# Cross-attention and routed FFN on one Trainium2 core: Q, K and V as seven of eight block products (Strassen, one level), in two phases with K and V kept in DRAM

## Chip, cores and metric

The kernel runs on one core of a Trainium2 chip. Times are device microseconds (us) of that core; three timed runs of the kernel before are given. It is written by hand: each engine has its own instruction stream, and semaphores are the only order between them. The names used below are those of the profile: PE is TensorE's matmul, PEld its weight load, DVE is VectorE, ACT is ScalarE, POOL is GpSimd, SP is SyncE, which issues every DMA here.

## What is computed

The reference, cut to what matters (B = 8 batches of 128 tokens, D = 512, 32 heads of 128):

```python
h = rmsnorm(layernorm(x)) * ln_weight          # 1024 x 512
q = h @ w_q.T;  k = ctx @ w_k.T;  v = ctx @ w_v.T      # each 1024 x 4096, 32 heads of 128
score = q k^T + position_bias[head]            # per batch and head, 128 x 128
score = where(mask, score, -inf); p = where(mask, softmax(score), 0)
x1 = x + layernorm(x) + (p v) @ w_out.T
y = layernorm(x1)
r = softmax(y @ gate_w.T)                      # 8 experts
out = x1 + ((y * (r @ in_scale)) @ sign(weight).T) * (r @ out_scale) + bias
```

## The kernel before, in words

Everything is f32. A projection is made of three fp32r matmuls per 128 rows of the inner dimension: each operand is split into a high part (an fp32r copy, by ACT) and a low part (operand minus high part, by DVE or POOL), and `three` (L740) issues high x high, low x high, high x low into one PSUM bank. The inner dimension is 512, so one bank of 128x512 results takes 4 x 3 = 12 matmuls of 128x512.

`schedule()` (L44) writes out one list of steps by hand; every engine walks this list (`walk`, L248) and issues what it has in each step, in that order. A step waits only through semaphores, but an engine that waits in one step holds back all its later steps. The steps that matter here:

- ("Q", h, half), ("K", h, half): `project` (L773), 12 matmuls for one head and four batches, into `proj_bank`; ACT copies the bank out (`evacuate`, L407). ("V", group, tile): the same for four heads and one batch.
- ("WQ", h), ("WK", h), ("WV", g): SP loads raw weights, ACT makes the high part (L404), POOL the low part (L343), except for the first ones, whose low part DVE makes (L524, L530).
- ("S", h, half): four f32 score matmuls of 128x128, each shown as two (L821). DVE adds bias and mask (L591) and takes the row maxima (L594), POOL having summed bias and mask before (L354). ("EXP"): four exponentials on ACT (L428). ("N"): DVE divides by the row sums (L600 to L603). ("T"): four transposes on PE (L830), copied by ACT (L437). ("PV"): probabilities times values (L841); ACT takes the high part (L443), DVE the low part (L609). One such run from S to PV is called a unit: 64 units, four per pair of heads.
- ("OUT", pair, b): 6 matmuls of the output projection for a pair of heads and one batch, into `out_bank` (two banks in turn), which DVE adds to the accumulator `acc` (L619).
- ("LN"), ("RMS"), ("H"), ("X"): the norms of x, eight transposes on PE and their splits, all within the first 60 us. ("SIGN"), and everything after ("ST", 0): the FFN.

Q, K and V of head h+1 stand between the units of head h, so that the products cover the latencies of the softmax. A steady slot holds, in PE's order, Q, S, Q, S, K, two OUTs, K, T, V, PV, T, V, PV. The weights of each head and the values of four heads are double buffered in SBUF; nothing intermediate goes to DRAM.

```python
for n, ((left_hi, left_lo), (right_hi, right_lo)) in enumerate(pairs):
    pe.matmul(bank_tensor[:], left_hi, right_hi, start=n == 0, stop=False)
    pe.matmul(bank_tensor[:], left_lo, right_hi, start=False, stop=False)
    last = pe.matmul(bank_tensor[:], left_hi, right_lo, start=False, stop=n == len(pairs) - 1)
```

## Time and profile before

| what | value |
|---|---|
| median of 3 runs | 937.71 us (935.98 to 940.04) |
| profiled execution, first to last instruction | 936.0 us (its own time outside the span is not listed) |
| PE busy | 902.8 us, 96% of the span |
| DVE, ACT, POOL busy | 386.1, 382.1, 266.5 us |
| mean granted TensorE clock | 0.993 |
| chain that ended last: PE | 85% of the span, of which the three projection lines 54% |
| HBM read, written | 42.25 MB, 2.10 MB |

The profile is of one execution. Busy times of PE overlap: a 128x512 matmul is shown with some 0.39 us, while the next one starts 0.23 us after it. Work on PE is therefore counted below by the distance of starts, not by busy time.

### The profile page before, as it was taken

The numbers are of one execution on the slowest core, as the hardware profiler recorded it, in microseconds if no ns is written. First come the engines' busy times: TensorE is split into PE (matmuls) and PEld (weight loads), VectorE is DVE, ScalarE is ACT, GpSimd is POOL, SyncE is SP. The second block draws the span as 40 slices with busy tenths as digits, with TensorE's granted clock in tenths as the row PEclk, the third lists the DMA queues.
The fourth block names the chain that finished last, engine by engine and source line by source line (L and its number), as shares of the span: only waits on it lengthen the run. The fifth ranks groups of instructions, "written<-read, shape, count | busy, mean of one in ns | idle before, by whom it ended". The sixth has DMA issues, their size and how long they took to land.

```text
span 936.0 us, 12277 instructions
## 1 busy us (share of the span) xinstructions
PE 902.8 (96%) x4590; PEld 754.5 (81%) x4590; DVE 386.1 (41%) x666; ACT 382.1 (41%) x998; POOL 266.5 (28%) x183
## 2 busy tenths in 40 slices
PE   8789999999999999999999999999999999999898
PEld 7668888787888878787887878788787878888775
DVE  6943333334243233424233332423333242365784
ACT  6345334342433435252343435343353424354552
POOL 1452115131331314331151323313142311233152
PEclk9999999999999999999999999999999999999998
DMA  9120002010020101111020101201012100120002
GB/s 326 42 71 29 34 26 91 28 49 15 26 80 25 48 26 48 60 29 41 16 94 26 48 17 39 78 12 49 26 48 71 42 22 12 48 68 26 1 3 88
DMA packets 22330, 45.15 MB, mean 48 GB/s; under 512 B 2536, under 2 KB 6888, under 8 KB 21248
## 3 DMA queue, kind: packets, MB, share of 16 engines
q1 hardware_dynamic: 22272, 44.36, 14.6%
q8 instruction: 38, 0.62, 0.3%
q14 instruction: 20, 0.16, 0.1%
HBM read 42.25 MB, written 2.10 MB: 47 GB/s over the span
## 4 chain that ended last, share of the span: by engine, by line
PE 85%; DVE 8%; issue 3%; ACT 1%; DMA 1%; SPq 1%; DVEq 0%; ACTq 0%
PE proj L745 18%; PE proj L751 18%; PE proj L748 18%; PE o L841 6%; PE s L821 6%; PE out L745 5%; PE out L751 5%; PE out L748 5%; PE t L830 3%; DVE acc L619 2%; DVE probs_t L571 1%; DVE inv_sum L602 1%; DMA acc<-in_x 1%; PE proj L909 1%; PE proj L910 1%
## 5 line engine op out<-in xcount | busy, mean ns | idle before, releaser
L609 DVE TENSOR_TENSOR o_lo<-o,o_hi 128x512 fp32r<-128x512 f32 x64 | 44.2, 691 | 268.3 <-ACT o_hi L443 268.3
L354 POOL TENSOR_TENSOR bias_mask<-bias_raw,mask_neg 128x512 f32<-128x512 f32 x64 | 75.0, 1172 | 270.9 <-DVE probs L591 264.5
L428 ACT ACTIVATE probs<-probs,neg_max 128x128 f32<-128x128 f32 x256 | 99.7, 391 | 121.0 <-DVE neg_max L594 120.9
L619 DVE TENSOR_TENSOR acc<-out,acc 128x512 f32<-128x512 f32 x128 | 87.1, 688 | 83.9 <-PE out L751 82.7
L745 PE MATMUL out<-wo_hi,o_hi 128*128 128x512 f32 x256 | 104.3, 407 | 15.1 <-DVE acc L619 13.4
L745 PE MATMUL proj<-wv_hi,c_hi 128*128 128x512 f32 x256 | 106.5, 416 | 0.0
L745 PE MATMUL proj<-c_hi,wk_hi 128*128 128x512 f32 x256 | 103.7, 405 | 1.3 <-ACT c_hi L421 1.3
L745 PE MATMUL proj<-x_hi,wq_hi 128*128 128x512 f32 x256 | 103.9, 406 | 0.0
L343 POOL TENSOR_TENSOR wq_lo<-wq_raw,wq_hi 128x512 fp32r<-128x512 f32 x33 | 48.2, 1460 | 194.1 <-ACT wq_hi L404 194.1
L751 PE MATMUL proj<-wv_lo,c_hi 128*128 128x512 f32 x256 | 101.3, 396 | 0.0
L748 PE MATMUL out<-wo_hi,o_lo 128*128 128x512 f32 x256 | 101.0, 394 | 0.0
L751 PE MATMUL out<-wo_lo,o_hi 128*128 128x512 f32 x256 | 101.0, 394 | 0.0
L748 PE MATMUL proj<-c_hi,wk_lo 128*128 128x512 f32 x256 | 100.9, 394 | 0.0
L751 PE MATMUL proj<-c_lo,wk_hi 128*128 128x512 f32 x256 | 100.7, 393 | 0.0
L748 PE MATMUL proj<-wv_hi,c_lo 128*128 128x512 f32 x256 | 100.6, 393 | 0.0
L748 PE MATMUL proj<-x_hi,wq_lo 128*128 128x512 f32 x256 | 99.9, 390 | 0.0
L751 PE MATMUL proj<-x_lo,wq_hi 128*128 128x512 f32 x256 | 99.8, 390 | 0.0
L415 ACT ACTIVATE q_sb<-proj 128x512 f32<-128x512 f32 x64 | 37.5, 586 | 134.8 <-PE proj L751 134.8
L415 ACT ACTIVATE v_sb<-proj 128x512 f32<-128x512 f32 x64 | 38.2, 597 | 113.0 <-PE proj L751 113.0
L415 ACT ACTIVATE k_sb<-proj 128x512 f32<-128x512 f32 x64 | 37.4, 585 | 111.4 <-PE proj L751 111.4
L591 DVE TENSOR_TENSOR probs<-s,bias_mask 128x512 f32<-128x512 f32 x64 | 44.0, 688 | 82.8 <-PE s L821 82.8
L745 PEld LDWEIGHTS out<-wo_hi,o_hi 128*128 128x128 f32 x256 | 48.3, 189 | 30.1 <-issue 20.5
(111 smaller groups left out, 1570.4 us busy)
## 6 DMA issues: line engine op xcount, KB each, us to landing
wk_raw<-in_wk SPq DMA_DIRECT2D x33, 256.0 KB, 2.9
wq_raw<-in_wq SPq DMA_DIRECT2D x33, 256.0 KB, 2.6
wo_raw<-in_wo SPq DMA_DIRECT2D x16, 512.0 KB, 3.3
wv_raw<-in_wv SPq DMA_DIRECT2D x7, 1024.0 KB, 4.7
bias_raw<-in_pos_bias SPq DMA_DIRECT2D x33, 64.0 KB, 2.1
v_sb<-in_ctx_t SPq DMA_DIRECT2D x8, 256.0 KB, 6.1
acc<-in_x SPq DMA_DIRECT2D x2, 1024.0 KB, 9.4
out<-acc SPq DMA_DIRECT2D x8, 256.0 KB, 2.0
```

Of the source, the lines that this page charges most:

```text
L343: pool.tensor_tensor(lo[:], raw[:], hi[:].bitcast(F32), ALU.subtract).then_inc(done, 1)
L354: pool.tensor_tensor(bias_mask[:, n % 2], bias_raw[:, None, :].to_broadcast([P, HALF, P]), mask_neg[:, halves[half], :], ALU.add).then_inc ...
L415: act.activation(to, proj_bank[order % 2][:], ACT.Copy).then_inc(a_proj, 1)
L428: last = act.activation(probs[:, n % 2, b, :], probs[:, n % 2, b, :], ACT.Exp, bias=neg_max[:, col:col + 1], accum_out=row_sum[:, col:col ...
L591: dve.tensor_tensor(probs[:, n % 2], s_bank[n % 2][:].rearrange("p (b k) -> p b k", b=HALF), bias_mask[:, n % 2], ALU.add).then_inc(v_scor ...
L609: dve.tensor_tensor(o_lo[:, h % 2, part], o_bank[:], o_hi[:, h % 2, part].bitcast(F32), ALU.subtract).then_inc(v_olo, 1)
L619: dve.tensor_tensor(acc[:, b, :], out_bank[n % 2][:], acc[:, b, :], ALU.add).then_inc(v_acc, 1)
L745: pe.matmul(bank_tensor[:], left_hi, right_hi, start=n == 0, stop=False)
L748: pe.matmul(bank_tensor[:], left_lo, right_hi, start=False, stop=False)
L751: last = pe.matmul(bank_tensor[:], left_hi, right_lo, start=False, stop=n == len(pairs) - 1)
L821: last = pe.matmul(to[:, b * P:(b + 1) * P], q_sb[:, h % 2, toks], k_sb[:, h % 2, toks], start=True, stop=True)
L841: last = pe.matmul(to[:, b * P:(b + 1) * P], v_sb[:, group % 2, half * HALF + b, j * P:(j + 1) * P], probs_t[:, n % 2, b * P:(b + 1) * P], ...
```

## The change

Q, K and V are each computed by one level of Strassen's scheme in Winograd's form: the 512 inner rows and the outputs are cut in two halves, and of the eight block products seven remain, on sums of blocks of the activations and of the weights. One **group** is 4 blocks of 128x512 results (a pair of heads for Q and K, both halves of the tokens; or four times 128 tokens by 512 columns for V), made of 7 products of 6 matmuls each: 42 instead of 48. There are 16 groups each of K, V and Q, 48 in all.

The seven products of a group go into two PSUM banks, which accumulate over products: bank 0 takes products 1, 2, 7, 4, bank 1 takes 6, 5, 3; only 1, 7 and 6 start afresh. After each product one engine reads the bank: ACT after 1 and 2 (steps E1, C11), DVE after 6, 5, 7, 3, 4 (E6, E65, C22, C12, C21), adding to a tile of `ring`. The sums of weights are made by POOL on the raw weights (`pair_sums`, `value_sums`), the splits of the sums by ACT (high) and, for K and V, DVE (low); for Q POOL makes the low part. The sums of the context and of x are made once by DVE and POOL.

The kernel now has two phases. **Phase 1**: the 32 groups of K and V of all heads; a cycle is one group, with seven places for products (slots 0 to 6), in which products of group k (1 in slot 0, 6 in 2, 2 in 4, 5 in 6) alternate with the late ones of group k-1 (7 in slot 1, 3 in 3, 4 in 5). Even groups use `proj_bank`, odd ones `out_bank`. Each of the four result tiles is stored to DRAM (`save`); x is loaded, normed, transposed and split only in the last nine cycles, four tiles at a time, and its residual passes through DRAM (`x_load`). **Phase 2**: per pair of heads, K and V are loaded back (`keys_and_values`, 1 MB each, two tiles of each), and the 7 products of Q (for the pair after the next), 4 units and 8 OUTs are interleaved in 4 slots, one per unit.

The diff, cut to its core (the rest renames tiles and semaphores and gives the loads their new shapes):

```diff
-                    three(to, pairs, pe_proj, before)
+READ = {1: "E1", 2: "C11", 7: "C22", 4: "C21", 6: "E6", 5: "E65", 3: "C12"}
+FIRST_BANK = (1, 2, 7, 4)
+STARTS = (1, 7, 6)
...
+        new = {0: 1, 2: 6, 4: 2, 6: 5}
+        old = {1: 7, 3: 3, 5: 4}
...
+        put(k, 3, ("WL", m + 1))
+        put(k, 5, ("WS", m + 1))
+        put(k, 6, ("WX", m + 1, 0))
+        put(k + 1, 0, ("WX", m + 1, 1))
+        put(k + 1, 2, ("WX", m + 1, 2), ("WX", m + 1, 3))
...
+        put(k + 1, 0, ("VX", g, 5), ("VS4", g))
+        put(k + 1, 2, ("VX", g, 7))
+        put(k + 1, 4, ("VX", g, 3))
+        put(k + 1, 6, ("VX", g, 4))
...
+    put(k - 3, 3, ("LN", 0))
...
+    put(k + 1, 3, ("X", 3), *[("XL", i) for i in range(HALF, B)])
+    put(k + 2, 1, ("LN", 1))
...
+        return [*nxt, *early, *bias, *load, ("T", j), *middle, *norm, *extra, ("PV", j), *late]
...
+        elif p < LAST:
+            o = p - 1
+            steps += slot(j, outs(o, 3, 4), prod[1], outs(o, 5), [*split(1)])
+            steps += slot(j + 1, outs(o, 6) + prod[6], outs(o, 7), prod[2], [*split(2, 3)])
+        if p < LAST:
...
+            steps += slot(j + 2, prod[5] + prod[7], prod[3], [], [("WO", p), ("WOL", p + 1), *load])
+            steps += slot(j + 3, outs(p, 0) + prod[4], outs(p, 1), outs(p, 2), [("KV", p + 2), *sums])
+        else:
+            o = p - 1
+            steps += [("SIGN", c) for c in range(2)]
+            steps += slot(j, outs(o, 3, 4), outs(o, 5), [], [("SIGN", 2)])
+            steps += slot(j + 1, outs(o, 6), outs(o, 7), [], [("SIGN", 3), ("WO", p), ("SCALES",)])
+            steps += slot(j + 2, outs(p, 0), outs(p, 1), [])
...
+            def save(n, name):
...
+                sp.wait_ge(*read_done(name, n))
...
+                    sp.dma_start(k_spill[index[0]][:, i, j * HT:(j + 1) * HT], tile).then_inc(d_save[n % 3], 16)
...
+            def x_load(i):
+                if i >= HALF:
+                    sp.wait_ge(g_r, i - HALF + 1)
+                    sp.dma_start(r_spill[i - HALF], x_tiles[:, i - HALF]).then_inc(d_r[i % HALF], 16)
+                    sp.wait_ge(d_r[i % HALF], 16)
+                sp.dma_start(x_tiles[:, i % HALF], x[i]).then_inc(d_x[i % HALF], 16)
...
+            def pair_sums(m):
...
+                pool.tensor_tensor(w_stage[:, 4], w_stage[:, 0], w_stage[:, 5], ALU.subtract).then_inc(g_wsum, 1)
...
+                pool.tensor_tensor(w_stage[:, 1], w_stage[:, 6], w_stage[:, 4], ALU.subtract).then_inc(g_wsum, 1)
...
+            def c21(n):
+                dve.wait_ge(pe_prod, nth_product[n, 4])
+                dve.wait_ge(*read_done("E6", n))
+                dve.tensor_tensor(ring[:, n % 3, 2], banks_of(n)[0][:], ring[:, n % 3, 2], ALU.add).then_inc(v_read, 1)
...
+            def product(n, i):
...
+                to = take(banks_of(n)[0 if i in FIRST_BANK else 1])
...
+                three(to, pairs, pe_prod, i in STARTS)
+                read_by(to, *read_done(READ[i], n))
```

Three places of the order are needed later. On **PE**, in the steady part, from a transpose of probabilities to the product with the values; before, twelve matmuls of a V step stand between them (the three rows shown come four times):

```order
L830 MATMUL t<-ident,probs 128x128 x3
L745 MATMUL proj<-wv_hi,c_hi 128x512 [waits g_wv_lo,a_proj]
L748 MATMUL proj<-wv_hi,c_lo 128x512
L751 MATMUL proj<-wv_lo,c_hi 128x512
...
L841 MATMUL o<-probs_t,v_sb 128x128 [waits v_olo,a_proj,a_pt]
L841 MATMUL o<-probs_t,v_sb 128x128 x3
```

and in the changed kernel, third slot of the first pair of phase 2, with what follows:

```order
L1110 MATMUL t<-ident,probs 128x128 x3
L1049 MATMUL proj<-x_hi,w_hi 128x512 [waits g_wlo,v_read]
L1050 MATMUL proj<-x_hi,w_lo 128x512
L1051 MATMUL proj<-x_lo,w_hi 128x512
...
L1121 MATMUL o<-probs_t,v_first 128x128 [waits v_olo,d_v0,a_pt]
L1121 MATMUL o<-probs_t,v_first 128x128 x3
L1102 MATMUL s<-k_second,ring 128x128 [waits v_score,d_k1,a_read]
L1102 MATMUL s<-k_second,ring 128x128 x3
L1049 MATMUL out<-wo_hi,o_hi 128x512 [waits v_read,v_olo,g_wo_lo]
```

Six matmuls now stand between transpose and PV, and in this slot only the next unit's scores between PV and the first OUT that needs the low part of its result (v_olo).

On **DVE**, before, one head of the steady part:

```order
L594 TENSOR_REDUCE neg_max<-probs 128x4 [waits v_score]
L619 TENSOR_TENSOR acc<-out,acc 128x512 [waits v_acc,pe_out]
L600 RECIPROCAL inv_sum<-row_sum 128x4 [waits a_exp]
L602 TENSOR_TENSOR inv_sum<-inv_sum,row_valid 128x4 [waits v_chain]
L603 TENSOR_TENSOR probs<-probs,inv_sum 128x512 [waits v_chain]
L619 TENSOR_TENSOR acc<-out,acc 128x512 [waits v_acc,pe_out] x3
L609 TENSOR_TENSOR o_lo<-o,o_hi 128x512 [waits a_ohi] x2
```

and now, a cycle of phase 1 in which values are split (v_lo, L829) between the reads of the banks:

```order
L800 TENSOR_TENSOR ring<-proj,ring 128x512 [waits a_read,pe_prod]
L829 TENSOR_TENSOR v_lo<-big_stage,v_hi 128x1024 [waits a_vhi]
L813 TENSOR_TENSOR ring<-out,ring 128x512 [waits pe_prod]
L829 TENSOR_TENSOR v_lo<-big_stage,v_hi 128x1024 [waits a_vhi]
L818 TENSOR_TENSOR ring<-out,ring 128x512 [waits v_read,pe_prod]
L804 TENSOR_TENSOR ring<-proj,ring 128x512 [waits pe_prod]
L825 TENSOR_TENSOR w_lo<-w_stage,w_hi 128x256 [waits a_whi]
```

Reads of products (L800 to L818) are new on this engine, and the splits of K and V stand in the same queue; L818 is C21, the last read of a group's bank 0, behind a split of 1024 elements.

On **SP**, the changed kernel where the second half of x is loaded:

```order
L452 DMA v_spill<-ring 128x2x256 x2
L468 DMA r_spill<-early 128x512
L470 DMA early<-in_x 128x512
...
L452 DMA v_spill<-ring 128x2x256 x4
L427 DMA w_stage<-in_wk 128x2x256
```

The pair r_spill, in_x comes four times; each in_x waits until its r_spill has landed. Before, x came in two loads at the start.

## Rows read from the trace of the kernel before

**Rows 1.** Page, part 1: busy time, share of the span, instructions.
```profile
PE 902.8 (96%) x4590; PEld 754.5 (81%) x4590; DVE 386.1 (41%) x666; ACT 382.1 (41%) x998; POOL 266.5 (28%) x183
```

**Rows 2.** Stages: length, busy by engine (instructions), PE clock, DMA share, GB/s.
```profile
10.00:20.00 10.00, 10.00 (x43) 8.22 (x42) 8.33 (x19) 7.29 (x13) 0.00 (x0) 1.00 1.05 403
...
30.00:40.00 10.00, 7.54 (x37) 5.72 (x36) 8.96 (x16) 3.59 (x8) 5.52 (x4) 1.00 0.05 15
40.00:60.00 20.00, 15.64 (x80) 12.66 (x79) 13.01 (x16) 6.89 (x12) 7.88 (x7) 1.00 0.07 22
60.00:80.00 20.00, 17.91 (x89) 14.92 (x88) 7.62 (x11) 10.65 (x27) 8.93 (x5) 0.91 0.26 85
...
200.00:300.00 100.00, 97.94 (x503) 82.35 (x502) 34.29 (x56) 36.43 (x95) 26.80 (x18) 1.00 0.15 45
```

**Rows 3.** Waits: engine, line, releaser: us in total, times, longest.
```profile
PE out L745 <- DVE acc L619: 13.4, 13, 1.0
```

**Rows 4.** PE's timeline, steady part: start, duration, line, op, tiles.
```profile
337.85 0.39 PE L745 MATMUL proj<-c_hi,wk_hi 128*128 128x512 f32 x1
...
340.57 0.60 PE L830 MATMUL t<-ident,probs 128*128 128x128 f32 x4
340.92 0.48 PE L745 MATMUL proj<-wv_hi,c_hi 128*128 128x512 f32 x1
```

**Rows 5.** Timeline of the start.
```profile
5.30 1.28 ACT L421 ACTIVATE c_hi<-v_sb 128x512 fp32r<-128x512 f32 x2 [0.98 <-DMA v_sb<-in_ctx_t]
...
6.07 0.77 PE L745 MATMUL proj<-c_hi,wk_hi 128*128 128x512 f32 x1 [1.30 <-ACT c_hi L421]
...
10.47 0.63 PE L748 MATMUL proj<-c_hi,wk_lo 128*128 128x512 f32 x1
```

**Rows 6.** Groups by form: busy us, mean ns | idle before them.
```profile
L619 DVE TENSOR_TENSOR acc<-out,acc 128x512 f32<-128x512 f32 x128 | 87.1, 688 | 83.9 <-PE out L751 82.7
L343 POOL TENSOR_TENSOR wo_lo<-wo_raw,wo_hi 128x1024 fp32r<-128x1024 f32 x16 | 38.1, 2379 | 7.9 <-ACT wo_hi L404 7.9
L404 ACT ACTIVATE wk_hi<-wk_raw 128x512 fp32r<-128x512 f32 x33 | 20.6, 623 | 1.7 <-DMA wk_raw<-in_wk 1.7
L518 DVE TENSOR_TENSOR c_lo<-v_sb,c_hi 128x512 fp32r<-128x512 f32 x8 | 5.4, 692 | 2.2 <-ACT c_hi L421 2.2
L543 DVE BATCH_NORM_STATS2 stats<-acc 128x6 f32<-128x512 f32 x8 | 4.9, 677 | 1.0 <-DMA acc<-in_x 1.0
```

**Rows 7.** Page, part 6: DMA issues, KB each, median us to landing.
```profile
wk_raw<-in_wk SPq DMA_DIRECT2D x33, 256.0 KB, 2.9
...
out<-acc SPq DMA_DIRECT2D x8, 256.0 KB, 2.0
```

**Rows 8.** Line 603 (two SBUF inputs): duration ns min/median/max.
```profile
L603 DVE TENSOR_TENSOR probs<-probs,inv_sum x64: 691/693/1619, 65.9 to 879.8; 128x512 f32<-128x512 f32 x64
```

**Rows 9.** Timeline near the end: scores to exponentials, transpose to low part.
```profile
859.32 1.05 PE L821 MATMUL s<-k_sb,q_sb 128*128 128x128 f32 x8
...
860.41 0.69 DVE L591 TENSOR_TENSOR probs<-s,bias_mask 128x512 f32<-128x512 f32 x1 [2.92 <-PE s L821]
...
861.86 0.40 ACT L428 ACTIVATE probs<-probs,neg_max 128x128 f32<-128x128 f32 x1 [1.23 <-DVE neg_max L594]
...
865.71 0.60 PE L830 MATMUL t<-ident,probs 128*128 128x128 f32 x4
...
866.35 0.60 ACT L437 ACTIVATE probs_t<-t 128x512 f32<-128x512 f32 x1 [1.23 <-PE t L830]
...
868.63 0.60 ACT L443 ACTIVATE o_hi<-o 128x512 fp32r<-128x512 f32 x1 [1.68 <-PE o L841]
...
869.26 0.69 DVE L609 TENSOR_TENSOR o_lo<-o,o_hi 128x512 fp32r<-128x512 f32 x1 [0.83 <-ACT o_hi L443]
```

**Rows 10.** PE's timeline after an idle gap of the start.
```profile
67.60 0.66 PE L830 MATMUL t<-ident,probs 128*128 128x128 f32 x4 [2.09 <-DVE probs L603]
...
69.02 0.63 PE L748 MATMUL proj<-wv_hi,c_lo 128*128 128x512 f32 x1
```

1010 lines of the change are left out of this document (618 added, 392 removed), and 4 rows, old and new, of the table steps.

## The prediction

> **What bounds the kernel now.** I read the page's busy times first: PE is busy for 902.8 of 936.0 us, no other engine for more than 41% [rows 1]. The stages say the same in time: a stretch of 100 us in the middle has 97.9 us of PE and about a third each of DVE, ACT and POOL, and DMA at 45 GB/s, while an early stretch shows that 403 GB/s can be moved [rows 2]. The list of waits then gives PE's only steady loss: 13 waits of about 1.0 us for DVE's addition to `acc` [rows 3], one per pair of heads. So time falls by what PE no longer has to issue, and rises by each wait put in its way. The reader should see in PE's timeline what one matmul is worth: twelve of a K step lie between 337.85 and 340.57, that is 0.227 us each (2.72 / 12), not the 0.39 us of the duration [rows 4]. PE loses more than this only at the start. Its first matmul is at 6.07 us; the first twelve run at half clock (durations of 0.63 at 10.47) and cost 0.2 us more each [rows 5]; and from 30 to 80 us it idles 2.5, 4.4 and 2.1 us [rows 2], waiting for the norms of x. With about ten gaps whose edges hide 0.16 us each (0.39 - 0.23) and 1.8 us for the clock of 0.91 in 60 to 80, the start costs 6.1 + 2.4 + 8.9 + 1.6 + 1.8 = 20.8 us.
>
> **The change, part by part.**
>
> *Removed.* 48 groups of 6 matmuls less: 288 x 0.227 = **-65.4 us**. All were on PE's path. The distance should stay: operands are still 128x128 against 128x512, from the same kinds of tiles.
>
> *Reads of the banks.* 48 x 5 on DVE, at the 0.69 us of the nearest row, a PSUM bank added to an SBUF tile [rows 6]: 165 us of new DVE work. In phase 1 a cycle is 42 x 0.227 = 9.5 us of PE; DVE has 3.5 us of reads and, per K group, 2.4 us of low parts (0.35 + 3 x 0.69). It fits on average. What counts is who waits. Most banks have three slots (4.1 us) before PE wants them again. C21 has one: product 4 in slot 5, product 1 of the group after the next in slot 0, with only product 5 (1.36 us) between. After the last matmul DVE needs about 0.2 + 0.69 us, so the slack is 0.4 us. In the cycles where values are split, a low part of 1024 elements stands ahead of C21. I estimate it at 1.25 us, below two of the 512-element row [rows 6] (bounds 0.7 and 1.4), behind an ACT high part of 1.1 that waits for C11. DVE starts C21 some 1.6 us late: a stall of 1.1 us in three such cycles, 3.3 us. The same place is blocked once by the four statistics of x (2.7 us with what follows 3.0, [rows 6]): 1.8 us, once by a wait for a root, 0.3, and once by a split of x: 1.1. Sum **+6.5 us**.
>
> *The second half of x.* SP stores a residual tile, waits for it to land (2.0 us [rows 7]), then loads; four times that is about 9.4 us with the issues, and the last load lands 2.6 later. It starts in slot 3 of cycle 24; LN for it stands in slot 1 of cycle 25, where DVE then waits until about 8 us into the cycle. Behind it wait E6 and C12, and behind these PE's product 5. **+3.8 us**. SP's stores of results, queued behind, are late by one cycle at most, and the ring has three groups: nothing.
>
> *DRAM.* 33.5 MB more are written and as much read. Phase 1 moves about 175 GB/s (1 MB stored and 0.5 MB or more loaded per 9.5 us), phase 2 about 110, against 403 seen [rows 2]. The loads of K and V come one pair (some 30 us) ahead. Nothing, unless an issue on SP is held; the bounds are 0 and one 5 us wait at the turn of the phases.
>
> *Start.* The first product needs the first context block, 1.1 us of high part and 1.25 of low part: about 7.5 us. After that DVE must make 6 low parts and 2 sums of 1024 elements and 4 weight splits (12.4 us) before PE can finish group 0, and only then does SP load the weights of K pair 1, which need 2.9 us [rows 7] and their splits: 23.5 us. By 31.5 us I count 11 products done, 15.0 us of work: 16.5 lost. Now POOL: it has 6 operations of 1024 elements in this stretch, 2.4 us each [rows 6]. Line 603, whose inputs are both in SBUF, takes 0.69 us in the median but 1.62 at most [rows 8]; the addition from PSUM keeps 688 ns over 128 times [rows 6]. So a DVE operation with two SBUF inputs can be held by POOL, for what POOL has left. The bounds are nothing and all 14.4 us; I take 6.5, since half of the operations would meet each other. Start: 23 us against the 20.8 that it replaces, **+2.2 us**.
>
> The Trainium skill, "SBUF — State Buffer", section "Who interferes with whom", says that a VectorE instruction with two SBUF inputs and a GpSimd instruction that reads SBUF exclude each other for a whole instruction. That rule speaks against this change, which puts all low parts of K and V on DVE beside POOL's sums; the trace agrees as far as its 1.62 us go. Without it the sum would be 6.5 us lower.
>
> *Steady part of phase 2.* A pair is 42 x 0.227 + 48 x 0.231 + 4 x 2.2 (units) = 29.4 us of PE. I follow one slot. Scores start at 0; DVE adds the bias at 1.1, ACT begins the exponentials at 2.5 and ends at 4.1 [rows 9]. PE transposes the unit before at 3.6, ACT can copy at 4.2 (0.64 after [rows 9]), just after the exponentials; the copy ends at 4.9 and PV starts at 5.4, after six matmuls. The shorter cover holds with half a microsecond. The third slot does not: its last step is PV, then only the next scores (0.8 us) and then OUT, which needs ACT's high part (1.1 us after the start of PV, 0.6 long) and DVE's low part (0.69) [rows 9], behind a division that itself stands behind C12, or POOL's low part of the output weights (2.4 us [rows 6]). OUT starts about 1.4 us late, once per pair: 15 x 1.4 = 21, against 15 x 1.25 with its hidden edge now [rows 3]. **+2 us**. DVE's work per pair (22 us of 30) covers the rest.
>
> *Last pair.* It has no products of its own: 20.6 us of PE. Signs and scales (5 us of DVE) stand between its units, the copy of the second transpose waits for exponentials (3 us), the first OUT for the low part (3 to 4 us). Against about 1 us now: **+5 us**, bounds 2 and 9.
>
> Sum: 936.0 - 65.4 + 6.5 + 3.8 + 2.2 + 2 + 5 = 890.1 us of span. The median of the runs lies 1.7 us above the span of the profiled execution, so **892 us**.
>
> **The rivals.**
>
> *All cover holds* (the forecast's stalls are absorbed: DVE operations follow at 0.67 us, POOL is seldom in the way). For it: PE hardly ever waits now. Against: the slacks above are below a microsecond. Then only start and last pair remain: 936.0 - 65.4 + 2 + 1.7 = 874; 872 to 880.
>
> *The clock drops.* After an idle gap of 2.1 us the trace shows matmuls of 0.63 us from 69.02 on, eight in all, 1.6 us lost [rows 10]; the granted clock of that stage is 0.91 [rows 2]. If each pair's stall did this, and the start ran at half clock throughout (5 us), it would be 892 + 15 x 1.6 + 5 = 921. Against: the steady waits of 1.0 us now leave the clock at 1.00. The Trainium skill, "TensorE: Matmul & The Clock Gate", section "A second HAM failure mode: psum-queue depth-cycling", tells of a kernel whose short idles between PSUM groups made the clock swing; the stages from 200 to 300 us do not show it here.
>
> *Slower: every bank read late.* If DVE, with splits, reads and softmax in one queue, ran behind all the time, PE would wait at each of 64 units and 32 cycles, at the 1.0 us of the one such wait now known [rows 3]: 874 + 96 + 5 = 975 us. It is slower than before from 0.65 us per slot or cycle. Against: DVE's sums, 60% of a K or V cycle and 75% of a pair. For: C21's slack of 0.4 us is in every cycle.
>
> *The change does not do what it says*: not so; the order holds 2016 projection matmuls where 2304 were. What is left is one long wait that I have not seen, such as K and V arriving late for each pair; 2 us in each would give 922.
>
> **How the numbers follow.** Forecast 0.64 (880 to 905), all cover 0.13, clock or late loads 0.15 (905 to 930), slower 0.05, something between 0.03. About 0.5% is what a measurement can tell, 4.7 us. Leaving out under 2 in 10, the range runs from 874 to 915. Faster 0.93, same 0.02, slower 0.05.
>
> **What would show it.** Distances of 0.227 us between product matmuls; a pair of phase 2 about 31 us from S to S, and one wait of PE's OUT for DVE's o_lo or POOL's wo_lo of about 1.4 us in it; in phase 1 a wait of product 1 for DVE's L818 in the cycles with v_lo; LN's statistics waiting for in_x by about 5 us near 250 us; PE half idle until 30 us. Wrong would be a DVE busy above 90% of a phase, a granted clock under 0.95 beyond the start, or cycles of phase 1 longer than 10 us throughout.

## The result, and the profile after

The changed kernel takes **1065.95 us** (median of 4 runs, 1064.63 to 1066.31) against 938.12 us of the kernel before in the same set: a ratio of 1.137, with a 95% interval of 1.1345 to 1.1389. The forecast was 892 us, within 874 to 915. The sign was wrong, and the miss is 174 us.

The page of the changed kernel: busy times, tenths in 40 slices, and the chain that ended last.

```profile
span 1064.1 us, 12773 instructions
PE 901.9 (85%) x4302; PEld 737.5 (69%) x4302; DVE 673.7 (63%) x992; ACT 386.1 (36%) x987; POOL 377.2 (35%) x326
PE   2889789889797877678898889988998889888788
DVE  5846445546663755146676767676766776676786
PEclk7899989899898989689999899998999999999899
PE 51%; issue 16%; DVE 11%; POOL 10%; DMA 8%; ACT 3%; SPq 1%; ACTq 0%; POOLq 0%; DVEq 0%
```

PE's busy time is as long as before [rows 1], though 288 matmuls are gone: a matmul at half clock is shown with 0.63 us, not 0.39, and some 270 of them run so, against 36 before. With the 0.2 us that the prediction gives to each of these, the half clock is some 47 us of the 174 (an estimate, 234 x 0.2). The clock (PEclk) is below full nearly everywhere, and PE, 85% of the chain before, is 51% of it now. No other engine is full. So the time is in waits, and in the clock behind some of them. The list of waits names them (us in total, times, longest):

```profile
POOL w_stage L545 <- DMA w_stage<-in_wk: 166.0, 15, 30.5
ACT w_hi L672 <- DMA w_stage<-in_wk: 70.5, 15, 7.8
PE out L1049 <- issue: 50.5, 16, 4.4
PE proj L1049 <- DVE w_lo L825: 23.1, 6, 7.3
PE out L1049 <- DVE w_lo L825: 14.0, 4, 4.5
PE proj L1049 <- POOL w_lo L557: 13.1, 2, 6.9
DVE stats L855 <- DMA early<-in_x: 8.8, 3, 3.0
```

The 7.3 us in this list are before the very first product, at 12.1 us; the longest wait for a low part after the start is 6.9 us. "Issue" stands where the profile names no releaser.

I compare three times with the forecast: that of C21 (L818) of the first group, the distances of C21 through phase 1, and the length of a pair. The 36 us for the first are the nine products before it (12.3 us), the 23 us that the prediction gives to the start, and the read.

| stretch | forecast, us | measured, us | difference |
|---|---|---|---|
| start to C21 of group 0 | about 36 | 46.7 | +10.7 |
| 31 more cycles of K and V | 305.8 | 394.3 | +88.5 |
| Q0 and Q1 at the turn of the phases | 19.1 | 38.2 | +19.1 |
| 13 steady pairs | 13 x 30.8 | 13 x 35.0 | +54 |
| rest (turn to pair 1, last two pairs, FFN) | | | +2, a balance |
| sum | 890.1 | 1064.1 | +174 |

**Phase 1.** A cycle without a weight split at its edge takes 9.3 to 9.8 us, as forecast. The cycles in which two K groups stand back to back take 14 to 20 us. One of them in the timeline (start, duration, engine, line, in brackets the idle time before it and its releaser):

```profile
405.14 0.55 SPq L427 DMA_DIRECT2D w_stage<-in_wk  x1
405.73 0.59 SPq L428 DMA_DIRECT2D w_stage<-in_wk  x1
409.71 0.42 ACT L672 ACTIVATE w_hi<-w_stage 128x256 fp32r<-128x256 f32 x1 [4.69 <-DMA w_stage<-in_wk]
410.16 0.60 DVE L825 TENSOR_TENSOR w_lo<-w_stage,w_hi 128x256 fp32r<-128x256 f32 x1 [2.27 <-ACT w_hi L672]
410.91 0.47 PE L1049 MATMUL out<-c_hi,w_hi 128*128 128x512 f32 x1 [3.75 <-DVE w_lo L825]
```

There is one buffer `w_stage`. SP may issue the next load, in two halves, only when the last low part of the pair before is made; both halves have landed 4.6 us after the first issue, and then the high part, the low part and PE's product 1 follow one behind the other. PE waits 3.75 us here, up to 6.9 elsewhere.

Twice the landing itself is slow: the loads issued at 124.3 and 208.2 us take 6.9 to 7.6 us, behind 2 MB of V's weights that SP had issued 3 to 4 us before them. The cycles that follow take 16.7 and 16.0 us, and in them the late low parts of K also meet GpSimd's sums of V (start, duration; PE's wait in brackets):

```profile
138.39 2.69 POOL L563 TENSOR_TENSOR big_stage<-big_stage 128x1024 f32<-128x1024 f32 x1
138.78 2.85 DVE L825 TENSOR_TENSOR tail_lo<-w_stage,tail_hi 128x512 fp32r<-128x512 f32 x1
142.88 0.80 PE L1049 MATMUL proj<-v_hi,c_hi 128*128 128x512 f32 x1 [3.11 <-DVE ring L818]
```

**Phase 2.** The third slot of a pair:

```profile
627.46 1.06 PE L1121 MATMUL o<-probs_t,v_first 128*128 128x128 f32 x8
627.88 2.35 POOL L618 TENSOR_TENSOR wo_lo<-wo_raw,wo_hi 128x1024 fp32r<-128x1024 f32 x1 [4.13 <-ACT wo_hi L748]
628.47 1.78 DVE L913 TENSOR_TENSOR inv_sum<-inv_sum,row_valid 128x4 f32<-128x4 f32 x1
630.19 1.15 POOL L613 TENSOR_TENSOR bias_mask<-bias_raw,mask_neg 128x512 f32<-128x512 f32 x1
630.29 1.60 DVE L914 TENSOR_TENSOR probs<-probs,inv_sum 128x512 f32<-128x512 f32 x1
631.81 0.68 DVE L921 TENSOR_TENSOR o_lo<-o,o_hi 128x512 fp32r<-128x512 f32 x1
632.59 0.47 PE L1049 MATMUL out<-wo_hi,o_hi 128*128 128x512 f32 x1 [3.18 <-issue]
633.37 0.60 PE L1049 MATMUL out<-wo_hi,o_hi 128*128 128x512 f32 x1
633.76 0.63 PE L1050 MATMUL out<-wo_hi,o_lo 128*128 128x512 f32 x1
```

DVE's division (L913 on 4 elements, then L914) runs beside two operations of POOL: L913 ends when the first does, and L914 has most of its own 0.69 us still to do when the second has ended. The low part of the output (L921) stands behind it and ends at 632.49, and the first OUT of the pair, which needs it, starts at 632.59 after a wait of 3.18 us; POOL's wo_lo had been ready since 630.23. Eight matmuls at half clock follow, two of which are shown. The row before for L914's work is the 0.69 of [rows 8].

### The profile page after: what moved, and what is told of

It reads as the page before. It is cut to its first block, busy times and chain, and to the rows that moved or that the text cites. A ratio compares the mean times of both kernels' runs of the same rounds, so it can differ in the third digit from the quotient of the medians.

```text
span 1064.1 us, 12773 instructions
## 1 busy us (share of the span) xinstructions
PE 901.9 (85%) x4302; PEld 737.5 (69%) x4302; DVE 673.7 (63%) x992; ACT 386.1 (36%) x987; POOL 377.2 (35%) x326
## 4 chain that ended last, share of the span: by engine, by line
PE 51%; issue 16%; DVE 11%; POOL 10%; DMA 8%; ACT 3%; SPq 1%; ACTq 0%; POOLq 0%; DVEq 0%
PE out L1049 9%; PE out L1051 8%; PE out L1050 8%; PE proj L1049 5%; PE proj L1050 5%; PE proj L1051 5%; DMA w_stage<-in_wk 4%; POOL wo_lo L618 4%; POOL w_lo L557 3%; PE o L1121 3%; PE s L1102 3%; POOL bias_mask L613 2%; DVE w_lo L825 2%; PE t L1110 2%; ACT w_hi L672 2%
## 5 line engine op out<-in xcount | busy, mean ns | idle before, releaser
L557 POOL TENSOR_TENSOR w_lo<-w_stage,w_hi 128x256 fp32r<-128x256 f32 (+1 forms) x64 | 72.7, 1145 | 173.3 <-ACT w_hi L672 173.0
L1049 PE MATMUL proj<-x_hi,w_hi 128*128 128x512 f32 x210 | 94.2, 449 | 13.2 <-POOL w_lo L557 13.1
L672 ACT ACTIVATE w_hi<-w_stage 128x512 fp32r<-128x512 f32 (+1 forms) x120 | 66.4, 568 | 100.8 <-DMA w_stage<-in_wk 70.5
L825 DVE TENSOR_TENSOR w_lo<-w_stage,w_hi 128x512 fp32r<-128x512 f32 (+1 forms) x56 | 50.3, 908 | 61.6 <-ACT w_hi L672 61.6
L1050 PE MATMUL proj<-x_hi,w_lo 128*128 128x512 f32 x210 | 88.2, 420 | 0.0
L1051 PE MATMUL proj<-x_lo,w_hi 128*128 128x512 f32 x210 | 86.7, 413 | 0.0
L1049 PE MATMUL proj<-c_hi,w_hi 128*128 128x512 f32 x112 | 50.7, 453 | 36.8 <-DVE w_lo L825 23.1
L914 DVE TENSOR_TENSOR probs<-probs,inv_sum 128x512 f32<-128x512 f32 x64 | 71.6, 1118 | 2.2
L618 POOL TENSOR_TENSOR wo_lo<-wo_raw,wo_hi 128x1024 fp32r<-128x1024 f32 x16 | 38.2, 2385 | 75.8 <-ACT wo_hi L748 75.8
L921 DVE TENSOR_TENSOR o_lo<-o,o_hi 128x512 fp32r<-128x512 f32 x64 | 43.8, 684 | 28.2 <-ACT o_hi L742 28.2
L1051 PEld LDWEIGHTS out<-wo_lo,o_hi 128*128 128x128 f32 x256 | 52.2, 204 | 12.5
L1050 PEld LDWEIGHTS out<-wo_hi,o_lo 128*128 128x128 f32 x256 | 52.2, 204 | 6.8
```

Source lines behind the costliest of these rows:

```text
L557: pool.tensor_tensor(lo, w_stage[:, STAGED[part]], hi.bitcast(F32), ALU.subtract).then_inc(g_wlo, 1)
L618: pool.tensor_tensor(wo_lo[:], wo_raw[:], wo_hi[:].bitcast(F32), ALU.subtract).then_inc(g_wo_lo, 1)
L672: act.activation(hi, w_stage[:, STAGED[part]], ACT.Copy).then_inc(a_whi, 1)
L825: dve.tensor_tensor(lo, w_stage[:, STAGED[part]], hi.bitcast(F32), ALU.subtract).then_inc(v_wlo, 1)
L914: dve.tensor_tensor(probs[:, j % 2], probs[:, j % 2], inv_sum[:, cols, None].to_broadcast([P, HALF, P]), ALU.mult).then_inc(v_probs, 1)
L921: dve.tensor_tensor(o_lo[:, h % 2, part], o_bank[:], o_hi[:, h % 2, part].bitcast(F32), ALU.subtract).then_inc(v_olo, 1)
```

## The experiments

Theories: **A**, the reload of the single weight buffer is late; **B**, GpSimd's operations hold VectorE's; **C**, idle waits lower the clock and so cost twice; **D**, the first OUT of a pair has too little work over its latency. A result without a range is the time of one run, so differences of a few us between two such results are not told apart; the kernel before took 934 to 940 us beside all of them. Savings are against the 1066.0 us of the changed kernel unless another is named.

### One part taken away

```diff
             def pair_weights(m):
+                if m:
+                    return
...
-                    act.wait_ge(d_w, 32 * (m + 1))
+                    act.wait_ge(d_w, 32)
```

> Only the weights of the first pair of K heads are loaded for Q and K; all later pairs reuse them, so the weights (and the 16 MB of loads) of the 31 other pairs are left out, and POOL's sums wait for the low parts alone. Theory A (the single weight buffer: the load of the next pair is issued late, lands 4 to 8 us later, ACT and DVE wait for it in order and PE behind them): PE's waits for DVE's w_lo (some 37 us) and for POOL's w_lo (some 18 us) and the half-clock matmuls behind them go, 1066 becomes about 1000, and cycles of phase 1 where K groups stand back to back fall from 15 to 20 us to about 10 to 11. Rival B (VectorE is held by GpSimd's operations while both read SBUF): the low parts stay as slow as they are, only the DMA's share goes, 1045 or more.

**1012.8 us**, 53 less: between the two expectations, nearer to A's. C21 of the last K group comes at 396.8 in place of 441.0; PE's waits for low parts of weights fall from some 55 to some 29 us. The back-to-back cycles take 10 to 14 us, and those of Q1 and Q2 16 and 17. A is the largest single cause of phase 1; pairs stay at 35 us. The edit takes away the late issue and the slow landing together and does not tell them apart.

```diff
-                pool.tensor_tensor(w_stage[:, 4], w_stage[:, 0], w_stage[:, 5], ALU.subtract).then_inc(g_wsum, 1)
+                c = slice(0, 2 * P if not m else 8)
+                pool.tensor_tensor(w_stage[:, 4, c], w_stage[:, 0, c], w_stage[:, 5, c], ALU.subtract).then_inc(g_wsum, 1)
...
```

> GpSimd's sums of weights of K, V and Q are cut to 8 columns from the second pair and the second group of V on (the rest of those sums is left out); all semaphores stay. Theory B (VectorE's low parts of 0.7 to 1.25 us take 2.8 to 3.4 us beside GpSimd's sums): no low part over 1.5 us in phase 1 after 60 us, and 1066 becomes 1025 to 1040. Theory A (the loads are late): the waits for the low parts stay, since GpSimd's 4 sums (3 us) are only the tail of a wait of 5 to 8 us; 1050 to 1060. Phase 2 should change by less than 10 us by either.

**1046.6 us**, 19 less: between the two expectations, a little nearer to A's. The two cycles behind the load at 124.3 us fall from 16.7 and 12.0 to 11.1 and 9.2 us, and those with a late load and no sums of V beside it nearly stay (15.9 and 15.4 us become 15.0 and 15.6). The cycle of 16.7 us fell to 11.5 with one load as well: there the two causes are links of one chain.

```diff
...
-                pool.tensor_tensor(wo_lo[:], wo_raw[:], wo_hi[:].bitcast(F32), ALU.subtract).then_inc(g_wo_lo, 1)
+                c = slice(0, D if not p else 8)
+                pool.tensor_tensor(wo_lo[:, :, c], wo_raw[:, :, c], wo_hi[:, :, c].bitcast(F32), ALU.subtract).then_inc(g_wo_lo, 1)
```

> In phase 2 GpSimd's low parts of the Q weights and of the output weights and its sums of bias and mask are cut to 2 or 8 columns (the rest is left out), semaphores stay; phase 1 is as it was. Theory D1 (GpSimd's long operations hold VectorE and come late themselves: wo_lo, 2.4 us, stands in the third slot of each pair): the wait of the first OUT of a pair (3.2 us) and the half clock after it go, a pair falls from 35 to about 31 us, 1066 becomes about 1005. Rival D2 (the order: only one score stands between PV of the third unit and the first OUT, so that ScalarE's high and VectorE's low part of the output are late by themselves): the wait stays at 1.4 to 2 us, a pair is 33 to 34 us, 1035 to 1050.

**1004.6 us**, 61 less, as D1 said: a pair takes 30.6 us and the wait of the first OUT 0.65 us in the steady pairs, less than the 1.4 of the forecast. So GpSimd's operations beside it are what made the slot longer than forecast. Two successive C21 show the pair, and the stage from 600 to 700 us the clock (columns as in [rows 2]):

```profile
615.30 0.69 DVE L821 TENSOR_TENSOR ring<-proj,ring 128x512 f32<-128x512 f32 x1 [0.71 <-PE proj L1054]
646.00 0.69 DVE L821 TENSOR_TENSOR ring<-proj,ring 128x512 f32<-128x512 f32 x1 [0.71 <-PE proj L1054]
600.00:700.00 100.00, 98.05 (x557) 83.90 (x556) 68.33 (x121) 50.46 (x157) 15.62 (x42) 1.00 0.28 99
```

### The order mended in phase 2

```diff
-            steps += slot(j + 1, outs(o, 6) + prod[6], outs(o, 7), prod[2], [*split(2, 3)])
+            steps += slot(j + 1, outs(o, 6) + prod[6], outs(o, 7), prod[2], [*split(2, 3), ("WO", p), ("WOL", p + 1)])
...
-            steps += slot(j + 2, prod[5] + prod[7], prod[3], [], [("WO", p), ("WOL", p + 1), *load])
-            steps += slot(j + 3, outs(p, 0) + prod[4], outs(p, 1), outs(p, 2), [("KV", p + 2), *sums])
+            here = [("WO", p), ("WOL", p + 1)] if p == 0 else []
+            steps += slot(j + 2, prod[5] + prod[7], prod[3], [], [*here, *load])
+            steps += slot(j + 3, prod[4] + outs(p, 0), outs(p, 1), outs(p, 2), [("KV", p + 2), *sums])
```

> Full computation. Product 4 of Q stands before the first OUT of the pair instead of behind it, and the split of the output weights stands one slot earlier. If the cover of the first OUT is what is short (1.4 us more of PE work now lies over it, and wo_lo is out of the way), the wait of 3.2 us falls below 1 us and the matmuls behind it run at full clock: a pair of 31 to 32 us, about 1015. If VectorE is simply late as a whole (it is held by GpSimd in every slot), the wait moves to another place in the pair and the time stays above 1050.

**999.2 us**, 67 less, and more than expected. No wait is left in a steady pair, which takes 29.8 us: the 29.4 of PE's work in the forecast and 0.4. The same stage has PE busy throughout at full clock:

```profile
614.55 0.68 DVE L819 TENSOR_TENSOR ring<-proj,ring 128x512 f32<-128x512 f32 x1
644.30 0.68 DVE L819 TENSOR_TENSOR ring<-proj,ring 128x512 f32<-128x512 f32 x1
600.00:700.00 100.00, 100.00 (x570) 85.98 (x569) 73.28 (x123) 52.13 (x164) 51.69 (x44) 1.00 0.30 104
```

POOL is as busy here as it would be in any correct version, so it need not be taken away: the edit moves its 2.4 us to a place where nobody waits, and puts 1.4 us more of PE's work over the chain of the output. Which of the two steps gave how much was not separated.

### What a removed matmul is worth

```diff
+                    if order > 24 and order % 2:
+                        pairs = pairs[:3]
```

> The kernel before, with 9 instead of 12 matmuls in every second projection step from the 25th on, so one quarter of the inner dimension is left out there; nothing else changes. There are 192 projection steps, 84 of them are cut: 252 matmuls fewer. If removed matmuls are worth their distance, 0.227 us, the time falls by 57 us, to about 882. If the kernel before were bound by something that PE's busy time hides (the chain per head, or the reads of the banks), it falls by less than 40.

**892.8 us**, 47.1 less where 57 were expected. The group of OUT's first matmuls shows the rest (busy, mean ns, idle before it):

```profile
L745 PE MATMUL out<-wo_hi,o_hi 128*128 128x512 f32 x256 | 104.4, 408 | 24.2 <-DVE acc L619 22.4 <-issue 1.7
```

That wait was 13.4 us [rows 3] and is 22.4: with less work between the OUTs they wait longer. 47.1 + 9.0 = 56.1, that is 0.223 us for each of the 252; PE's other waits are as long as before to within 0.5 us. The first term of the forecast holds, and a part of it is lost where matmuls were cover.

### VectorE beside GpSimd, alone

```diff
+                    last = pool.tensor_tensor(pool_out[:, i], xt[:, 4:6], xt[:, 6:8], ALU.subtract)
...
+                    return dve.tensor_tensor(v_out[:, i], xt[:, 0:2], xt[:, 2:4], ALU.subtract)
```

> None of the computation is done: six copies each of five VectorE instructions alone, then beside six GpSimd additions of 1024 elements, both inputs of GpSimd in SBUF. Theory B (an instruction of VectorE with two SBUF inputs and one of GpSimd exclude each other): alone 1024 elements take about 1.2 us and 512 take 0.69; beside GpSimd (2.4 us each) they wait for it, 2 us or more on average, and the form from PSUM plus SBUF keeps 0.69, a form with one input keeps its time. Whether a 4-element instruction is held (1.6 us at times in phase 2) shows in the last group. Rival: they only share the bandwidth: every form, one input too, becomes some tens of per cent longer and none takes over 2 us.

Runs of one form each (start, time of all, count). L72 has two SBUF inputs of 1024 elements, L74 of 512, L76 a PSUM and an SBUF input, L78 one SBUF input of 512, L79 one of 4; the first row is VectorE alone, the others are beside GpSimd:

```profile
11.62 7.02 DVE L72 TENSOR_TENSOR v_out<-xt 128x1024 f32<-128x1024 f32 x6
21.84 9.91 DVE L72 TENSOR_TENSOR v_out<-xt 128x1024 f32<-128x1024 f32 x3
27.36 9.88 POOL L59 TENSOR_TENSOR pool_out<-xt 128x1024 f32<-128x1024 f32 x3
46.21 8.31 DVE L74 TENSOR_TENSOR v_out<-xt 128x512 f32<-128x512 f32 x3
65.64 6.79 DVE L76 TENSOR_TENSOR v_out<-ps,xt 128x512 f32<-128x512 f32 x11
70.50 9.25 POOL L59 TENSOR_TENSOR pool_out<-xt 128x1024 f32<-128x1024 f32 x4
88.36 10.00 DVE L78 TENSOR_SCALAR v_out<-xt 128x512 f32<-128x512 f32 x4
106.61 9.20 DVE L79 TENSOR_SCALAR v_out<-xt 128x4 f32<-128x4 f32 x7
```

With two SBUF inputs VectorE's instruction of 1024 elements takes 3.3 us beside GpSimd and 1.2 alone, and GpSimd's takes 3.3 as well, against 2.3 beside the form from PSUM: they take turns, and each is shown with the other's time. The form from PSUM keeps its 0.6 to 0.7 us (the first of the 11 in its row still run alone). Against my expectation the form with one SBUF input is held too (2.5 us against 0.4), and so is one of 4 elements: in turn one takes 2.3 us, about GpSimd's own, and the next 0.16, which is 1.3 on average. What is paid is the rest of GpSimd's instruction, not a share of one's own size. The Trainium skill, "SBUF — State Buffer", section "Who interferes with whom", has both cases, the second as a mode of `tensor_scalar` that uses two ports; the times agree with it, though the trace does not show the mode.

### The order mended in phase 1

```diff
+            order = order + v[0:1] + KEYS[k:k + 1] + v[1:2] + KEYS[k + 1:k + 2] + v[2:4] + KEYS[k + 2:k + 3]
...
-        put(k, 3, ("WL", m + 1))
+        e = k - 1 if 2 <= m < NPAIR and at[KEYS[m - 1]] < k - 1 else k
+        put(e, 3, ("WL", m + 1))
```

> Full computation. The order of the first 24 groups of phase 1 never has two K groups behind each other, and the load of a pair's weights is issued a cycle earlier where there is one to spare; the edit of phase 2 (product 4 before the first OUT, the split of the output weights a slot earlier) is kept, with which the time was 999.2. Theory A (the load of the single weight buffer is late where K groups stand back to back): the cycles of 15 to 17 us of the first 24 groups fall to 10 to 12, five of them, so 25 to 30 us less: about 972. Those from K12 to Q1 stay at 15 to 20. If the splits of V's weights, held by GpSimd's sums, make these cycles long (rival B), they stay above 13 us, and the time above 985.

**964.6 us**, 34.6 less than the 999.2 of the order mended in phase 2, which is kept here. From the second to the 24th group the cycles are 9.3 to 13.0 us long; those from K12 to Q1 keep their 12 to 21. A again.

The next kernel moved all of phase 1's sums and low parts to VectorE:

```diff
-                pool.tensor_tensor(w_stage[:, 4], w_stage[:, 0], w_stage[:, 5], ALU.subtract).then_inc(g_wsum, 1)
+                dve.tensor_tensor(w_stage[:, 4], w_stage[:, 0], w_stage[:, 5], ALU.subtract).then_inc(g_wsum, 1)
...
-                pool.tensor_tensor(big_stage[:, 4], big_stage[:, 2], big_stage[:, 3], ALU.add).then_inc(g_vsum, 1)
+                dve.tensor_tensor(big_stage[:, 4], big_stage[:, 2], big_stage[:, 3], ALU.add).then_inc(g_vsum, 1)
```

> Full computation. As the kernel with the new order of groups and the later OUT, and in phase 1 all sums and low parts of context, weights and x stand on VectorE, none on GpSimd: about 1.2 us instead of 2.4 to 3.3 for 1024 elements, and no collision. Theory B: VectorE does more and still ends earlier; the start is 5 to 8 us shorter, the cycles with splits lose 1 to 2 us each, about 950 to 960. Rival (VectorE's queue is what is full, not its port): the start becomes 5 us longer and the reads of the banks come late: 975 or more.

**965.2 us**: no difference, so neither expectation. The start is 0.6 us shorter and the first cycle 2.2, but those of K12 to K14 are 1.2 to 2.0 longer (16.95 in place of 15.0). I read this as the pair's sums now standing in VectorE's queue behind the wait for the load; that was not tested.

### The clock alone

```diff
+                if b == 0 and p < LAST:
+                    for _ in range(10):
+                        pe.matmul(take(out_bank[n % 2])[:], x_hi[:, 0, 0, 0:P], x_hi[:, 0, 0, :], start=True, stop=True, skip_group_check=True)
                 pe.wait_ge(g_wo_lo, p + 1)
```

> The changed kernel with ten matmuls more (128x512, into the bank that the first OUT of a pair takes and overwrites) before the waits of that OUT, in 15 pairs; all else as in the change. They fill 2.3 of the 3.2 us in which PE waits there. Theory C (it is the idle wait that lets the granted clock fall, and the half-speed matmuls behind it cost 2.4 us per pair on top of the wait): no matmul of 0.63 us behind the first OUT, a granted clock of 1.00 in the stages of phase 2, a pair of 32 to 33 us in place of 35, about 1030 in all. Rival: the clock falls for what PE did over the whole pair, or the 2.4 us are not additional (the products behind would wait anyway): 1060 or more.

**1047.7 us**: 18 less for 150 matmuls more, in the middle between the 1030 of C and the 1060 of its rival. A pair takes 33.2 us, 1.8 less, and the granted clock is 1.00 from 500 to 800 us; in the changed kernel it is 0.95 in the stage shown:

```profile
655.46 2.52 PE L1130 MATMUL out<-x_hi 128*128 128x512 f32 x10
658.92 0.47 PE L1049 MATMUL out<-wo_hi,o_hi 128*128 128x512 f32 x1 [0.94 <-issue]
600.00:700.00 100.00, 97.19 (x546) 82.62 (x545) 73.66 (x113) 45.62 (x141) 45.42 (x40) 1.00 0.28 99
```

C is shown for the pairs: nothing that the OUT waits for was changed, and only the clock behind it has. Of the 5.6 us that a pair had over its work, at least 1.8 are the clock and 3.2 the wait itself. The 13 steady pairs alone gain 23 us; from C21 of the last Q group to the end this run takes 5 us longer than the changed kernel, and why was not followed.

### Small edits towards a better version

Each of these is made to the kernel of 964.6 us or its successor. First, ScalarE's first bank read moved forward:

```diff
-    steps = [("WARM",), ("WS", 0), ("CX", 1), ("WX", 0, 0), ("CX", 2), ("WX", 0, 1), ("CT", "T3"), ("CT", "T1"), ("CX", 7),
+    steps = [("WARM",), ("WS", 0), ("CX", 1), ("WX", 0, 0), ("CX", 2), ("WX", 0, 1), *product(0, 1)[:2], ("CT", "T3"), ("CT", "T1"),
+             ("CX", 7), ("P", 0, 2), ("C11", 0), ("CT", "T2"), ("WX", 0, 2), ("CX", 6), ("CT", "T4"), ("CX", 5), ("WX", 0, 3),
```

> Full computation; to the kernel of 964.6 us (groups alternated, OUT later) one edit: ScalarE reads the bank after the first product of the first group as soon as its queue has the second split of the context, not behind all seven splits, and the second product follows. Theory: PE's wait of 10.5 us for that read (from some 13 to 22 us) is due to its place in ScalarE's queue; the second product comes some 8 us earlier, later products then wait for the splits, and the start is 3 to 8 us shorter: 957 to 962. Rival (VectorE's low parts set the start): under 2 us.

**967.5 us**: nothing gained. The 10.5 us wait went, and one of 7.8 us for DVE's L807 and others of 1.7 and 2.3 us for its low parts stand in its place. VectorE's low parts set the start, as the rival had it. Then the load in two halves:

```diff
+            def first_weights(m):
+                if m:
+                    for part in range(2):
+                        sp.wait_ge(*low_done(m - 1, part))
+                    sp.wait_ge(g_wsum, 4 * m)
+                sp.dma_start(w_stage[:, 0:3:2], w[2 * (m % NPAIR)].rearrange("p (b c) d -> p b (c d)", b=2)).then_inc(d_wa, 16)
```

> Full computation; to the kernel of 964.6 us one edit: the raw weights of the first head of a pair are loaded as soon as the first two splits of the pair before are done, by a DMA of their own, and only those of the second head after the last split. Theory A (late loads into the single buffer are what the cycles from K12 to Q1 of 12 to 20 us consist of): product 1 no longer waits for the load (5 us), the wait moves to product 6, which has 1.4 us more cover, and the six cycles lose 2 to 4 us each: 945 to 952. Rival (the chain of sums, high and low parts is as long by itself): under 5 us less, 960 or more.

**956.6 us**, 8 less than 964.6: just under the 960 of the rival, and short of theory A's 945 to 952. Two cycles fell from 16 and 15 to 12.5 us, the others changed by 1.4 at most. Both edits together:

> Full computation; groups alternated, OUT later, early read and split load together. If their gains add (7 and 16 us), about 942, within 1% of the kernel before (938 to 940); if the rivals hold for both, 960.

**957.8 us** (957.6 to 960.7), ratio to the kernel before 1.0224, interval 1.0203 to 1.0244: the early read adds nothing. It was left out of what follows.

With the three causes taken away at once (loads, sums, the order of phase 2; the same edits as above):

> The changed kernel with three edits together: weights of Q and K loaded once (those of the other pairs are left out), GpSimd's sums cut to 8 columns (the rest of the sums left out), and the order of phase 2 with the later OUT. If the loads, the sums on GpSimd and the cover of the first OUT are nearly all of what the forecast missed, their savings add or do better where one hid the other: 1066 - 67 - 53 - 19 = 927 or less, down to 905, with cycles of phase 1 of 9.5 to 11 us from 60 us on except the one in which VectorE waits for the second half of x. If a fourth cause of size is hidden behind them (the reads of the banks, DRAM traffic of the results), 940 or more.

**928.8 us**, 137 less: almost the sum of the single savings (139), just above what the three causes alone would give and well under the 940 of a fourth of their size. The 31 cycles take 342.1 us in place of 394.3, and Q0 and Q1 23.9 in place of 38.2. The cycle near 300 us keeps its 18.9, and nine late cycles take 11 to 14 us. That cycle is the second half of x; in the changed kernel:

```profile
317.53 1.65 SPq L468 DMA_DIRECT2D r_spill<-early  x1
320.98 0.35 SPq L470 DMA_DIRECT2D early<-in_x  x1
321.37 0.43 SPq L468 DMA_DIRECT2D r_spill<-early  x1
325.13 0.33 SPq L470 DMA_DIRECT2D early<-in_x  x1
328.05 0.69 DVE L855 BATCH_NORM_STATS2 stats<-early 128x6 f32<-128x512 f32 x1 [3.02 <-DMA early<-in_x]
328.71 0.33 SPq L470 DMA_DIRECT2D early<-in_x  x1
335.21 0.69 DVE L855 BATCH_NORM_STATS2 stats<-early 128x6 f32<-128x512 f32 x1 [2.92 <-DMA early<-in_x]
336.44 0.69 DVE L800 TENSOR_TENSOR ring<-out,ring 128x512 f32<-128x512 f32 x1
337.18 0.80 PE L1049 MATMUL out<-c_hi,w_hi 128*128 128x512 f32 x1 [7.89 <-DVE ring L800]
```

Store, wait, load takes 3.6 to 4.2 us a tile, and DVE follows tile by tile with a read of the bank (L800) behind it, for which PE waits 7.89 us. The next run mends it in the kernel of 956.6 us:

```diff
+                if i == HALF:
+                    for t in range(HALF):
+                        sp.wait_ge(g_r, t + 1)
+                        sp.dma_start(r_spill[t], x_tiles[:, t]).then_inc(d_r[t], 16)
                 if i >= HALF:
-                    sp.wait_ge(g_r, i - HALF + 1)
-                    sp.dma_start(r_spill[i - HALF], x_tiles[:, i - HALF]).then_inc(d_r[i % HALF], 16)
                     sp.wait_ge(d_r[i % HALF], 16)
```

> Full computation; to the kernel of 956.6 us one edit: SyncE issues the four stores of the residual first and then the four loads of the second half of x, instead of store, wait, load four times in turn. Theory: the three waits of VectorE's statistics for x (2.9 us each) and the 3.5 to 4 us steps of that queue are a round trip per tile; together the last load lands about 7 us earlier, and the cycle of 19.2 us becomes 11 to 14: 949 to 952. Rival (the wait moves to GpSimd's residual sums or the norms behind): within 2 us of 956.6.

**943.8 us**, 12.8 less, more than expected: the cycle falls from 19.2 to 10.9, and the two behind it by 1.9 and 1.6. SP's saves and loads stand behind the round trips in its queue, which may be why; that was not followed. With the sums of V and of the context on VectorE besides:

> Full computation; all edits that gained, and the sums of V's weights and of the context on VectorE (1.2 us each) in place of GpSimd (2.4 us and more), those of Q's and K's weights on GpSimd. If the gains add, 944 to 950, still 0.5 to 1.5% above the kernel before; if VectorE's queue becomes the limit in the cycles with V's splits, 955.

**938.2 us** (10 runs, 933.2 to 942.5), ratio 1.0003, interval 0.9984 to 1.0021: faster than the expected 944 to 950, and no difference to the kernel before that can be told. Last, the low parts of the first Q weights:

```diff
             def query_weights_low(m, part):
-                if m < NPAIR:
+                if m < NPAIR + 3:
                     return
```

> Full computation; to the kernel of 938.2 us one edit: the low parts of the first three pairs of Q weights are made by VectorE, as those of K are, and not by GpSimd, where the first of them stands behind the four sums of the pair. Theory: at the turn of the phases product 1 of Q waits 6.2 us for GpSimd's low part, of which 2.8 us are the sums; four cycles of 15 to 20 us lose about 2 to 3 us each: 930 to 933, 0.5 to 0.8% below the kernel before. Rival: the load is what it waits for, whoever makes the low part: 937 or more, no difference to the kernel before.

**928.9 us** (922.9 to 930.9), ratio **0.9907**, interval 0.9879 to 0.9935: the mended change is 0.9% faster than the kernel before, a little better than expected. The three cycles at the turn of the phases fall from 18.9, 16.9 and 19.6 to 14.9, 15.1 and 15.4 us, and PE's wait of 6.2 us there to 1.8. The stage from 60 to 400 us has a clock of 0.99 where the changed kernel has 0.93 (first row: this version, second: the changed kernel):

```profile
60.00:400.00 340.00, 316.42 (x1361) 250.86 (x1359) 220.10 (x312) 103.77 (x176) 77.22 (x82) 0.99 0.50 165
```

```profile
60.00:400.00 340.00, 289.18 (x1182) 228.35 (x1180) 191.42 (x256) 88.23 (x141) 88.90 (x72) 0.93 0.40 134
```

## Why the prediction was wrong, step by step

- **Removed, -65.4: right.** The distance stayed 0.23 us at full clock, and the matmuls taken from the kernel before gave 0.223 each. The cover that goes with them cost 9 us there, and was counted in the forecast only as stalls of the new kernel.
- **"DRAM ... Nothing, unless an issue on SP is held": the step that failed in phase 1.** The load of the weights was looked at for its bandwidth and, at the start only, for its "2.9 us" [rows 7]. It was never followed through a cycle: one buffer, an issue that waits for the last low part, 4.6 us until both halves have landed and up to 7.6 behind V's weights, then ACT, DVE and PE in a row. Taking it away gave 53 us, an order that hides it 35, and its split in two loads 8. The stated bound, "one 5 us wait at the turn of the phases", was far too low: PE has three waits there of 17.7 us in all, and more before it. "It fits on average" was true of DVE (43 to 72% busy by stage) and beside the point.
- **Steady pair, +2: the place was right, the cost wrong, and this was as dear as the loads.** A pair took 35.0 us and not 30.8, 54 us over 13 pairs. The wait of the first OUT was forecast at 1.4 us and measured at 3.2. The 2.4 us of POOL's wo_lo were named as a cost in parallel; that POOL also holds DVE's division (1.78 and 1.60 us for 0.16 and 0.69) was priced at the start and left out here. With POOL shortened the wait is 0.65; with the order mended and POOL in full the pair is at 29.8 us.
- **The clock.** It was a rival at 921 us, argued against because "the steady waits of 1.0 us now leave the clock at 1.00". That reading holds, for 0.94 us too, and does not reach to 3.2 us, behind which the matmuls run at half clock. The filled wait shows at least 1.8 us per pair, so the rival's 1.6 was about right, and it came on top of the wait; its chance hung on the size of the wait. The prediction's own sign of being wrong, a granted clock under 0.95 beyond the start, came: 0.93 from 60 to 400 us and 0.85 from 400 to 500. Matmuls of 0.63 us stand behind late loads there too; what they cost in phase 1 was not tried by itself. The Trainium skill, "TensorE: Matmul & The Clock Gate", section "A second HAM failure mode: psum-queue depth-cycling", tells of a kernel whose short idles between groups make the clock swing; here it falls once per pair, behind a wait of 3.2 us, and in the run with ten matmuls more it does not.
- **Reads of the banks, +6.5: right in kind, too small.** PE waits five times for L818, 11.1 us in all. One wait behind a split of V is 1.1 us and one behind the statistics of x 1.4, near the forecast's 1.1 and 1.8. The waits at 142.9 and 226.2 us are 3.1 each, behind low parts of K that the late load had shifted to beside GpSimd's sums of V (with one load they are 1.1 and 0.5); the run with short sums took some 5 us from each of the two cycles.
- **Second half of x, +3.8: mis-sized.** The round trips were taken as 9.4 us and the last load as 2.6 more; from the first store to the last statistics it is 17.7 us, and PE waits 7.89. Mending it gave 12.8 us.
- **Start, +2.2: mis-sized by 10 us.** By 31.5 us PE was at the end of the third product, where eleven had been counted. The port collisions came as expected (2.8 to 3.4 us for low parts of 0.7 and 1.2), PE's first matmul came at 12.1 us and not at 7.5, and 27 of the first 60 matmuls ran at half clock. Moving the sums of V and the context to DVE brought C21 from 46.6 to 42.8.
- **Last pair, +5: waits too small, total about right.** The last two pairs have no products; PE's waits from 960 to 1020 us add to 14.8 us, the longest 4.4. Yet the stretch in which they lie is only some 2 us over the forecast (last row of the first table); what gave the difference back was not followed, so this part of the forecast was luck as far as it is known.
- **"Every bank read late" (975 us)** was the only case on the slow side, and it did not happen: DVE is 63% busy. Slower came otherwise. The nearest to it was "one long wait that I have not seen, such as K and V arriving late for each pair", at 922 us: late it was, but the weights and not K and V, and not once per pair.

What stays open: with the three causes away, 928.8 us is still 37 above the forecast. By the rows of the first table that is +10.7 for the start, +36.3 for the 31 cycles of K and V, +4.8 for Q0 and Q1 and -1 for the rest, while the 13 pairs of 29.7 us give back 14. So it lies in phase 1: the start, the cycle with the second half of x (18.9 us), and cycles of 11 to 14 us with splits, whose parts were not separated.

## What to carry to other kernels

When work moves from the engine that is full to those that are not, count buffers before bandwidth: for each buffer that is reloaded, write down release, issue, landing, the operations behind it, and the place at which the full engine wants them, for one whole cycle and for the tightest pair of neighbours. Price every operation with SBUF inputs that stands beside a long GpSimd operation at the rest of that operation, wherever it occurs. And when a wait of some microseconds appears on TensorE, add the half-speed matmuls behind it; where the wait can't go, its order often can, as one exchanged step and one moved split were worth 67 us here.

## What the runs showed of the hardware beyond that

A 4-element VectorE instruction took up to 1.8 us beside GpSimd in the kernel and 2.3 in the small one, against 0.16 alone. Beside a VectorE instruction with two SBUF inputs, GpSimd's 1024-element subtraction took 3.3 us instead of 2.3, so it is slowed in its turn. A 256 KB load of weights took 2.9 us from issue to landing in the kernel before (median), and 3.3 (K) and 4.0 us (Q) in the changed one, up to 7.6 behind two loads of 1 MB. Ten useless matmuls in a 3.2 us wait made the whole kernel 18 us faster.
